# Asking for a unit's rows six units ahead instead of four, in the expert stage of a GNN and mixture-of-experts kernel

## The reference, cut to what matters

```python
x = x + gnn(layernorm(x), adj, ...)          # x: 128 graphs x 128 nodes x 128 features
# mixture of experts, on 16384 tokens of 128 features, 8 experts with a hidden size of 512
xf = layernorm(x).reshape(-1, D)
top_w, top_i = top_k(xf @ Wg + bg, 2)        # two experts a token
top_w = softmax(top_w)
for e in range(8):
    h = gelu(xf @ W1[e] + b1[e])
    out += weight_of(e) * (h @ W2[e] + b2[e])
x = x + out
```

## Time and profile before

| what | value |
|---|---|
| three runs | 737.33, 737.63, 738.52 us |
| span of the profiled execution | 738.4 us (no other time is listed for it; it lies within the three runs) |
| TensorE busy | 657.4 us (89%), weight loads 598.6 us |
| VectorE, ScalarE, GpSimd busy | 617.8, 525.4, 500.8 us |
| DMA | 148.47 MB, mean 201 GB/s |
| unit rows | 140 loads of 260 KB, median 3.7 us from issue to landing |
| weights in the second stage | 50 loads of 512 KB |

### The profile page before, as it was taken

The page is one execution under the profiler, slowest core; times in us unless marked ns, Lnnn a source line. Parts: engine busy times, 40 slices in busy tenths (PEclk is TensorE's granted clock), DMA queues, the critical chain, the costliest instruction groups (busy, mean ns, idle before and its releaser), DMA issues.

```text
span 738.4 us, 17622 instructions
## 1 busy us (share of the span) xinstructions
PE 657.4 (89%) x4878; PEld 598.6 (81%) x4878; DVE 617.8 (84%) x2056; ACT 525.4 (71%) x1470; POOL 500.8 (68%) x469
## 2 busy tenths in 40 slices
PE   6879888998873979999998999999999999999990
PEld 4646666666562879888998999998999999999990
DVE  4899999999997658777887888887888888888881
ACT  5689999999961646666666767766767767767760
POOL 2652767767767857675776776777777777777773
PEclk9999999899955889999999999999999999999996
DMA  8999994547223567599569655499764444444310
GB/s 296 348 369 275 352 324 152 195 147 313 95 87 109 184 175 249 196 339 320 166 213 356 189 163 156 138 325 378 226 168 120 131 122 121 131 124 119 102 40 29
DMA packets 82040, 148.47 MB, mean 201 GB/s; under 512 B 32247, under 2 KB 36352, under 8 KB 81936
## 3 DMA queue, kind: packets, MB, share of 16 engines
q1 hardware_dynamic: 62576, 100.37, 44.3%
q0 software_dynamic: 18496, 46.70, 17.5%
q10 hardware_dynamic: 864, 0.21, 0.1%
HBM read 92.37 MB, written 57.23 MB: 203 GB/s over the span
## 4 chain that ended last, share of the span: by engine, by line
PE 58%; ACT 18%; DMA 8%; DVE 6%; issue 4%; POOL 3%; SPq 1%; POOLq 0%; ACTq 0%; DVEq 0%
PE bank L1391 8%; PE bank L1403 8%; PE bank L1392 8%; PE bank L1393 8%; PE bank L1408 8%; PE bank L1404 8%; DMA row<-rows 7%; ACT hs L687 5%; ACT row L696 5%; PE bank L1377 4%; ACT t_loop L678 4%; PE bank L1419 4%; ACT t_in L671 3%; POOL rows L591 2%; PE bank L1277 1%
## 5 line engine op out<-in xcount | busy, mean ns | idle before, releaser
L756 ACT ACTIVATE act_f<-bank,b_t 128x256 f32<-128x256 f32 x560 | 220.0, 476 | 7.8 <-PE bank L1393 1.6
L637 POOL DMA_INDIRECT rows<-row,to_row x140 | 167.2, 1194 | 74.0 <-issue 51.9
L634 POOL DMA_INDIRECT out_dram<-row,to_row x140 | 168.0, 1200 | 60.2 <-issue 56.4
L591 POOL DMA_INDIRECT rows<-row,slot_low x128 | 136.4, 1066 | 64.5 <-issue 34.8
L1228 DVE TENSOR_TENSOR act_lo<-act_f,act_hi 128x1024 fp32r<-128x1024 f32 x140 | 171.6, 1225 | 4.8
L746 ACT ACTIVATE in_hi<-bank 128x256 fp32r<-128x256 f32 x140 | 53.9, 385 | 154.9 <-PE bank L1377 154.9
L1223 DVE CAST act_hi<-act_f 128x1024 fp32r<-128x1024 f32 x140 | 97.8, 699 | 69.8 <-ACT act_f L756 69.6
L1391 PE MATMUL bank<-in_hi,w_t 128*128 128x256 f32 x376 | 113.5, 302 | 0.0
L1392 PE MATMUL bank<-in_lo,w_t 128*128 128x256 f32 x376 | 105.5, 281 | 0.0
L1393 PE MATMUL bank<-in_hi,w_t 128*128 128x256 f32 x376 | 105.5, 281 | 0.0
L1403 PE MATMUL bank<-act_hi,w_t 128*128 128x256 f32 x376 | 101.2, 303 | 0.2 <-DVE act_hi L1223 0.2
(11 more groups left out here) (225 smaller groups left out, 1658.9 us busy)
## 6 DMA issues: line engine op xcount, KB each, us to landing
row<-rows SPq DMA_DIRECT2D x140, 260.0 KB, 3.7
w_t<-w_split SPq DMA_DIRECT2D x38, 512.0 KB, 6.7
w_up<-w_split SPq DMA_DIRECT2D x18, 512.0 KB, 7.0
xs<-in_x_dram SPq DMA_DIRECT2D x16, 512.0 KB, 5.0
x_t<-in_x_turned_dram SPq DMA_DIRECT2D x16, 512.0 KB, 6.2
rows<-ends_rep SPq DMA_DIRECT2D x15, 260.0 KB, 7.8
b_t<-in_biases_dram SPq DMA_DIRECT2D x140, 2.5 KB
rows<-row,to_row POOLq DMA_INDIRECT x140, 3.7
```

The costliest lines, as they stand in the source:

```text
L591: pool.indirect_dma_start(out=rows, out_offset=bass.IndirectOffsetOnAxis(ap=slot_low[:, r, b:b + 1], axis=0), in_=row[:, r, b, :], in_offs ...
L634: pool.indirect_dma_start(out=out_rows, out_offset=at, in_=got[:, g, j, P:2 * P], in_offset=None, bounds_check=TOKENS - 1, oob_is_err=Fals ...
L637: pool.indirect_dma_start(out=rows, out_offset=at, in_=got[:, g, j, :], in_offset=None, bounds_check=NROWS - 1, oob_is_err=False).then_inc ...
L756: last = act.activation(act_f[:, s, c, :], ps_h(t, half)[:, i, :], ACT.Gelu, bias=b_t[:, w, c:c + 1])
```

## The change

The rows of a unit are asked for in turn k-6 instead of turn k-4, and six instead of four before the turns begin. `EARLY[0]`, the unit from which on all chunks must have landed, stays 8; `EARLY[1]`, the number of second-pass units with a need of their own in the table, goes from 12 to 14, so that it ends at the same turn as before. The wait for the first late chunk stays at unit 4. `AHEAD` also shifts the column of the unit table from which SP takes a row's address (L784) and the number of table entries that SP loads ahead of its lists (L504, L535, L537). Slots, engines' work, transfers and their sizes are the same.

```diff
-    WR, BR, GR, AHEAD = 3, 8, 16, 4
-
-    EARLY = [2 * AHEAD, 3 * AHEAD]
+    WR, BR, GR, AHEAD = 3, 8, 16, 6
+
+    EARLY = [8, 8 + AHEAD]
...
-        assert GR * BLK == 4 * G and (PART - 1) % RING == 1 and GR == 4 * AHEAD
+        assert GR * BLK == 4 * G and (PART - 1) % RING == 1 and EARLY[0] * BLK == 2 * G and AHEAD <= EARLY[0]
...
             def wait_landed(k, needs):
                 if k < EARLY[0]:
-                    if k == AHEAD:
+                    if k == 4:
                         sp.wait_ge(s_land, 2)
```

## The result

With rows asked for six units ahead the median is 733.2 us (729.8 to 737.7), beside 738.2 us (735.6 to 742.0) for the kernel before on the same chip: a ratio of 0.9923, 95% interval 0.9896 to 0.9951. The kernel got faster by 5 us; 9.2 were forecast, to 728.4 with 733.0 as the upper end of the range. The median lies 0.2 us above that end; the ratio, taken on the 737.6 us from which the forecast started, gives 731.9, inside it. The profiled execution has a span of 730.0 us and a time of 732.05 us.

What follows compares the result with a forecast made beforehand. TensorE was taken to wait for rows queued behind weights on full DMA engines in four stretches. 13.3 us regained, less 3.8 for weights and scatters and 0.3 at the start, gives 9.2: 737.6 to 728.4 us, range 724.5 to 733.

Steps and rivals of the forecast that it cites:

- What binds before: After the start, TensorE's transposes wait for rows queued behind weight loads in four expert-changing stretches, 13.3 us in all.
- The gain in the stretches: In the four stretches where units change expert and fetch weights, 13.3 us of row waits go, less 3.8.
- The term for weights: Late weights make PE wait 1.7, 0.6 and 1.3 us in stretches two to four: 3.6 us in all.
- I leave each weight load landing when it landed: In the four stretches DMA engines stay full, so weight landings were kept at their old times; 3.6 us of waits follow.
- The argument that full engines keep order: Against later weight landings in the stretches: full DMA engines keep order and bytes, so landings need not move.
- its first rival: Weights land later in the stretches as PE crowds the DMA engines: 735.9 us at 2 us later; chance 0.15.
- one of my signs of a wrong prediction: Weight landings of 8 us and more in the fourth stretch would show the prediction wrong.
- The start: First units: the later first GELU is hidden, unit 4's late biases mostly so; 0.3 us lost, bounds 2 us either way.
- a cover behind POOL's mark: Before unit 7's transposes PE stood 4.69 us until the first stage's last chunk was scattered; this hides the 1.5 us.
- The GELU term: At the start, two more row requests and table entries ahead of the first biases delay the first GELU 1.5 us.
- unit 4's GELU behind 264: At the start, unit 4's biases land at 264.3 behind the wait for unit 7's rows; its GELU ends at 265.9.
- The slots and the second pass: Row slots free 3.5 us before needed, unit 78's second-pass condition met 1.0 us early: both cost nothing.

Runs made afterwards that it cites:

- the fourth slot: A fourth weight slot per layer instead of three: on the changed kernel (six ahead) 730.03 us, ratio 0.9868; on the kernel before (four ahead) 742.50 us, ratio 1.0046.
- half loads: Changed kernel, rows six ahead, with each weight load bringing only 256 of its 512 KB: 725.26 us, ratio 0.9807 to the kernel before.

## Why the prediction was right, and where its size was off

*What binds before.* Right. No wait for rows is left in the stretches with six or five ahead, and none with four where no weights are fetched.

*The gain in the stretches: 13.3 less 3.8, so 9.5 us.* Measured from the means of the profiles, 14.0 - 5.9 = 8.1 us. The term for weights was too small, 3.6 forecast against 5.9:

| stretch | forecast | three profiles |
|---|---|---|
| 1 | 0 | 0.0, 0.1, 0.0 |
| 2 | 1.7 | 3.5, 3.2, 2.6 |
| 3 | 0.6 | 1.3, 1.6, 0.7 |
| 4 | 1.3 | 1.3, 1.2, 2.0 |

The step that failed is "I leave each weight load landing when it landed". The rate did stay, but in the second stretch unit 26's load landed 1.5 us later (1.4 and 0.9 in the other two profiles, by the moment at which PE went on). Of the 1.5 us, scatters sent sooner are some 0.3 us (0.2 were put down for them); the rest goes with what SP asked for behind the load and was moved before its last part. The argument that full engines keep order, which the prediction held against its first rival, did not hold there. The 1.5 us are the bulk of 3.3 - 1.7 = 1.6 us by which unit 26's load was later than forecast in the profile that shows its landing (wanted at 318.2 + 5 x 3.258 = 334.5, landed at 337.8). In the third stretch unit 43's load came 0.5 us later in the first profile (384.60 + 8.8, 21.9 us behind the stretch's first load; before 389.20 + 8.2, 21.4), about the amount by which that stretch lost more than the 0.6 forecast. In the fourth stretch loads took 8 us and more, one of my signs of a wrong prediction, and yet the stretch lost about what was forecast: unit 79's load, issued at 503.17, landed after 8.9 us, 38.3 us behind the stretch's first load, where it was 518.3 - 479.9 = 38.4 before. (In the third profile, where this stretch lost 2.0 us, it was 39.1.) The sign was badly chosen; a landing has to be counted from the first load and not from its own request.

The rule of the Trainium skill that I had weighed ("DMA: Bandwidth & Descriptors", Issuing engines are not separate DMA queues) says that DMAs started by different engines all run on the same 16 DMA engines and interleave. The runs agree: 351 GB/s on both sides, with SP's and POOL's transfers mixed. That asking earlier brings no bandwidth was the prediction's own conclusion from it, and it held in these windows; its first rival, later landings, came out in the second stretch, in part in the third, and not in the first profile's fourth.

*The start.* Forecast: 0.3 us lost, made of a first GELU 1.5 us later and a cover behind POOL's mark. The GELU term was right (246.72 - 237.66 = 9.1 us from SP's first request to ACT; before, 245.01 - 237.67 = 7.3), and so was unit 4's GELU behind 264 or nearly so (263.2). Missed was the mark of the weights that stand behind the same request: 2.6, 1.3 and 2.6 us of PE in the three profiles. That the start as a whole came out near the forecast all the same is luck. Counted from SP's first request for rows to unit 12's transposes, four profiles with rows four ahead (the two of before, and those without loads and with the fourth slot) have 40.9 to 44.8 us, mean 42.9; six with six ahead (the three, without loads, with half loads and with the fourth slot) have 41.8 to 43.9, mean 43.1. An effect of 0.3 us can't be told from that spread, and part of what was won and lost here is the clock: from 264 to 268 it was granted at 0.50 and 0.83 in the first two profiles, and at 1.00 in the second profile of before.

*The slots and the second pass.* Costed at nothing, and right for six ahead. Eight ahead shows that both margins were real and about as wide as forecast: two turns more use them up.

*The time.* 733.2, 732.8 and 731.6 us against 728.4. The gain by medians is 5.0, 7.2 and 6.3 us in the three comparisons, by ratio 3.6 to 7.7 in the first; the profiles give 8.1 us less 0.2 for the start. Of the 2 to 4 us that are missing from the forecast 9.2, 1.4 are the weights' late landing net of a larger loss before. The rest was not settled. In the profiles the first stage ends up to 5.5 us earlier or later (SP's first request for rows between 237.5 and 243.0 us), which no part of the change touches, and the intervals leave room for it. The time also lies 1.7 to 3.5 us above the span in the profiles, where I had taken it to be none. The kernel before, too, was slower in these comparisons (738.2, 740.0 and 737.9 us) than the 737.6 from which the forecast was taken off.

## What to carry to other kernels

When a wait goes away, ask what was queued behind it in time, and don't leave the next transfer landing when it landed: on full DMA engines here some loads kept their place within 0.1 us and one came 0.9 to 1.5 us later, by a small part (an estimated 0.3 us) since a faster engine sent its own output sooner, and while more of the requests made after it were moved. Count such a landing from the first request of the busy stretch and not from its own. More lead is worth something only until the wait changes hands; here one turn did it, two brought nothing more, and eight ahead ran SP into waits that had nothing to do with the one removed. In a list that is worked in order, every item behind a blocked request counts, increments without a transfer too.

## What the runs showed of the hardware

A stretch with more requests in flight moved its bytes at the same 351 GB/s, so a load of 512 KB that took 7.5 us took 10.8 us at an unchanged rate. On one issuing queue order was not kept to the byte: 0.7 to 1.0 MB that SP asked for behind this load were moved before its last part.

A granted clock of 0.50, the lower of TensorE's two levels (1.2 GHz), near 264 us does not belong to the kernel before as such. Its first profile has it; the second has these rows instead, the stretch in the columns of the earlier trace rows and unit 7's transposes:

```profile
264.00:268.00 4.00, 4.00 (x37) 4.00 (x36) 2.35 (x5) 3.04 (x9) 3.08 (x4) 1.00 0.83 230
...
262.94 0.44 PE L1377 MATMUL bank<-ident,row 128*128 128x128 f32 x2 [1.99 <-DMA row<-rows]
```

PE stood idle before these transposes in both, 4.69 us in the first and 1.99 us in the second. What makes the clock fall in the one and not in the other, these runs don't show.
